# The experts' gathered rows turned by a transposing DMA in place of TensorE

## The chip, the cores and the metric

The kernel runs on one core of a Trainium2 chip. Its time is the device time of one execution in microseconds (us), and what is compared is the median of several runs. A profiled execution gives the trace. TensorE does matrix products and turns tiles (a turn is a product with the identity matrix), VectorE (DVE) and ScalarE (ACT) do elementwise work and read TensorE's results out of its eight banks, GpSimd (POOL) issues the indirect transfers here, SyncE (SP) the plain ones.

## The reference

One decoder layer with three parts, each followed by a residual sum and a layer norm: causal self-attention, cross-attention with rotary positions, and a mixture of experts. The change touches only the last:

```python
x = hidden_states.reshape(-1, 512)                     # 2048 tokens of 512
scores = jax.nn.sigmoid(x @ gate_w.T) + bias
topk_w, topk_idx = jax.lax.top_k(scores, 4)            # 4 of 16 experts for each token
topk_w = topk_w / (jnp.sum(topk_w, axis=-1, keepdims=True) + 1e-20)
cw = jnp.sum(jax.nn.one_hot(topk_idx, 16) * topk_w[..., None], axis=1)
g, u = jnp.einsum('th,eih->eti', x, Wg), jnp.einsum('th,eih->eti', x, Wu)   # 256 wide
zw = jax.nn.silu(g) * u * cw.T[:, :, None]
out = jnp.einsum('eti,ehi->th', zw, Wd)
out = out + jax.nn.silu(x @ Sg.T) * (x @ Su.T) @ Sd.T  # shared expert
```

## The kernel before, in words

Every product is made in three passes of float16: each operand is split into a high and a low half, and high x high, high x low and low x high are summed in a bank (`three_pass`, L284). The profile therefore shows three matmuls, L288, L289 and L290, wherever a product stands.

The stages run one after the other: self-attention, cross-attention, routing with the shared expert, the experts, and a last stage that adds up and normalises. Routing has written the token rows to `scratch_x`; a row there holds 512 high halves, 512 low halves and the four weights of the token. It has also made lists that place the chosen (token, expert) pairs in 79 tiles of 128 rows, each tile of one expert.

The experts' stage (`experts`, L1847) is a loop over these 79 tiles, unrolled, and each engine has its own copy of it. In step s:

- TensorE does the gate and up products of tile s (`gate_and_up`, 12 matmuls) into bank `GU[s % 2]`; turns the rows of tile s + 2, which makes the left operands of a later step (`turn_rows`, L1462, 8 matmuls, high halves into bank `XH`, low halves into `XL`); does the down product of tile s - 1 (`down`, 6 matmuls); and turns z of tile s (`turn_z`, 2 matmuls).
- ScalarE makes silu of the gate (L1948), reads the number of expert weights that must have landed for tile s + 2 and waits for them, copies `XH` to `xth` (L1954), in every second step scales the output of tile s - 1 (L1957), and copies z's high half (L1959).
- VectorE makes z (L1972), copies `XL` to `xtl` (L1976), forms the weights of tile s + 2 (L1979, L1981), scales the outputs of the other steps (L1985), and makes z's low half (L1987).
- GpSimd gathers the rows of tile s + 4 into one of four slots of `rows` (L1456, 128 rows of 2064 bytes), and then sends the scaled output of tile s - 1 to HBM with an accumulating indirect transfer (L1934), which also waits for the accumulating transfer two tiles back.
- SyncE loads expert weights into a ring of four (L1452, 1.5 MB each), each load when the one before has landed and TensorE has done with the slot.

`xth` and `xtl` have two buffers each, so the operands of tile s + 2 go where those of tile s were read. A `Timeline` is a semaphore with an order of events written out by hand: `mark` counts an event, `value` is the count at which it has happened, and the engine marks them in exactly this order. ACT's queue is in order: what stands behind a waiting instruction waits too.

Of the kernel before, what the change touches and what calls it, by code (L numbers as in the profile page):

```python
# [108 lines left out]
def build(nc, x, xT, cT, maskf, wqT, wkT, wvT, b3, woT, bo, xwq, xwk, xwv, xwo,  # L109
# [3 lines left out]
    with top:  # L113
# [3 lines left out]
        def sem(name):  # L117
            return top.enter_context(nc.semaphore(name))
# [1310 lines left out]
        def moe_buffers(where):  # L1429
# [4 lines left out]
            m.rows, m.s_rows = b("rows", [P, 4, ROW], F16), [sem(f"moe_rows{j}") for j in range(4)]  # L1434
            m.xth = [b(f"xth{p}", [P, KD, ST], F16) for p in range(2)]
            m.xtl = [b(f"xtl{p}", [P, KD, ST], F16) for p in range(2)]
            m.list = b("list", [P, COLS], U32)
# [412 lines left out]
        def experts(m, ln):  # L1850
# [3 lines left out]
            with ExitStack() as ctx:  # L1854
# [6 lines left out]
                s_yo = [sem(f"mo_s_yo{j}") for j in range(U)]  # L1861
                XH, XL, GU, ZT, Y = bank[0], bank[1], [bank[2], bank[3]], [bank[4], bank[5]], [bank[6], bank[7]]

# [4 lines left out]
                AC = Timeline(sem("mo_act"), per_step(["si", "xh", "y", "zh"], 1), 0, [], U)  # L1868
                DV = Timeline(sem("mo_dve"), per_step(["z", "xl", "wp", "ws", "y", "zl"], 0), 0, [], U)
                assert LAST.q % 2  # L1870
# [41 lines left out]
                def _(pool):  # L1912
                    routing.gpsimd(pool)
                    routing.wait(pool, routing.PE, "turn1")
                    for s in range(NTILES + 1):
                        st = step(s)
                        if s >= 2 and s + U < NTILES:
                            pool.wait_ge(PE.sem, PE.value("turn", st, 2))
                            pool.wait_ge(DV.sem, DV.value("ws", st, 2))
                        elif s < 2:  # L1920
                            routing.wait(pool, routing.DV, f"ws{s}")
# [18 lines left out]
                def _(act):  # L1940
# [4 lines left out]
                    for s in range(NTILES):  # L1945
                        st, par = step(s), s % 2
                        act.wait_ge(PE.sem, PE.value("gu", st))
                        AC.mark(act.activation(sg[par][:, :], GU[par][:, 0:FI], ACT.Silu, scale=1 / WS), "si", st, () if turns(s) else ("xh",))  # L1948
                        if turns(s):
                            loaded = act.value_load(m.need[0:1, s + 2:s + 3], min_val=16, max_val=16 * NE)  # L1950
                            act.wait_ge(m.s_w, loaded)
                            met(act)
                            act.wait_ge(PE.sem, PE.value("turn", st))
                            AC.mark(act.activation(m.xth[par][:, :, :].rearrange("p k t -> p (k t)"), XH[:, :], ACT.Copy), "xh", st)  # L1954
                        if out_of(st) is AC:
                            act.wait_ge(PE.sem, PE.value("y", st))
                            AC.mark(act.activation(stored(act, s - 1)[:, :], Y[(s + 1) % 2][:, :], ACT.Copy, scale=weight(act, s - 1)), "y", st)  # L1957
                        act.wait_ge(PE.sem, PE.value("zt", st))
                        AC.mark(act.activation(zh[par][:, :, :].rearrange("p n t -> p (n t)"), ZT[par][:, 0:FI], ACT.Copy), "zh", st)  # L1959
# [6 lines left out]
                def _(dve):  # L1966
                    routing.vector(dve)
                    DV.start(dve)
                    for s in range(NTILES):
                        st, par = step(s), s % 2  # L1970
                        dve.wait_ge(AC.sem, AC.value("si", st))
                        i = dve.scalar_tensor_tensor(z[par][:, :], GU[par][:, FI:2 * FI], OS / WS, sg[par][:, :], ALU.mult, ALU.mult)  # L1972
                        DV.mark(i, "z", st, () if turns(s) else ("xl", "wp", "ws"))
                        if turns(s):
                            dve.wait_ge(PE.sem, PE.value("turn", st))
                            i = dve.tensor_copy(m.xtl[par][:, :, :].rearrange("p k t -> p (k t)"), XL[:, :])  # L1976
                            DV.mark(i, "xl", st)
                            t = s + 2
                            DV.mark(dve.tensor_tensor(m.of_pick[:, t % 2, :], weights_of(m, t), m.which[:, t, :], ALU.mult), "wp", st)  # L1979
                            dve.wait_ge(DV.sem, DV.value("wp", st))  # L1980
# [11 lines left out]
                def _(pe):  # L1992
# [7 lines left out]
                    def gate_and_up(s, w):  # L2000
# [5 lines left out]
                        else:  # L2006
                            pe.wait_ge(AC.sem, AC.value("xh", st, 2))
                            pe.wait_ge(DV.sem, DV.value("xl", st, 2))
                        n = 2 * FI
# [4 lines left out]
                        mm = three_pass(pe, GU[par][:, :], pairs[2:], start=False)  # L2014
                        PE.mark(mm, "gu", st, () if turns(s) else ("turn",))
                        return following
# [20 lines left out]
                    for s in range(NTILES):  # L2037
                        st = step(s)
                        following = gate_and_up(s, w)
                        if turns(s):  # L2040
                            t = s + 2
                            if s == 0:
                                routing.wait(pe, routing.DV, "to")
                            pe.wait_ge(m.s_rows[t % U], t // U * 16 + 16)
                            pe.wait_ge(AC.sem, AC.value("xh", st, 1))
                            pe.wait_ge(DV.sem, DV.value("xl", st, 1))
                            mm = turn_rows(pe, m, t % U, XH, XL)
                            PE.mark(mm, "turn", st, ("y",) if s == 0 else ())
                        if s:
# [228 lines left out]
```

## Time and profile before

| | us |
|---|---|
| median of 3 runs | 1805.72 (1804.32 to 1809.44) |
| profiled execution, its time | 1802.7 |
| its span in the trace | 1800.9 |
| TensorE busy | 1703.9 (95%) |
| VectorE busy | 1321.3 (73%) |
| ScalarE busy | 921.6 (51%) |
| GpSimd busy | 892.8 (50%) |
| experts' stage | about 1392 to 1762 |

The 40 slices of the page are 45 us each, so the experts' stage is about slices 32 to 39. A matmul of 512 columns is shown with 379 ns, but matmuls are pipelined: the start of the next one comes 216 ns later, and this distance is what it costs. The DMA share is the mean busy share of the 16 DMA engines that carry all queues.

### The profile page before, as it was taken

What the parts mean: (1) busy time and instruction counts of PE and PEld (TensorE: products, weight loads), DVE (VectorE), ACT (ScalarE), POOL (GpSimd) and SP (SyncE); (2) the same over time, 40 slices, a digit from 0 to 9 for tenths busy, and PEclk for the clock granted to TensorE, in tenths of its full rate; (3) what the DMA queues carried; (4) which work ended last, traced back from release to release, by engine and by line L of the source; (5) the groups of instructions that cost most, each with busy time, mean ns of one, the idle gap of its engine ahead of it and who ended that gap; (6) DMA issues with size and microseconds to landing.
All of it is one profiled execution on the core that took longest, in us unless ns stands there. A gap on an engine that the chain in (4) does not pass through costs nothing. (4 is left out here: it accounts for less than half of the span.)

```text
span 1800.9 us, 38771 instructions
## 1 busy us (share of the span) xinstructions
PE 1703.9 (95%) x15285; PEld 984.0 (55%) x15285; DVE 1321.3 (73%) x2251; ACT 921.6 (51%) x1545; POOL 892.8 (50%) x728
## 2 busy tenths in 40 slices
PE   6999999799999999999999999999899999899990
PEld 4676766455555555555555555555454555455550
DVE  4788789678888888888888888888879444344445
ACT  4566656755646464556465645565631333333335
POOL 7743032554646454646464555465531555455550
PEclk8999999999999999999999999999999999999996
DMA  9620010211413222214122122121244678787668
GB/s 283 143 49 20 8 62 3 95 66 42 141 53 107 77 71 94 89 46 143 53 89 77 53 92 73 48 94 59 77 160 141 153 153 221 201 224 153 116 103 298
DMA packets 84945, 190.40 MB, mean 106 GB/s; under 512 B 10848, under 2 KB 29664, under 8 KB 82720
## 3 DMA queue, kind: packets, MB, share of 16 engines
q1 hardware_dynamic: 61104, 129.44, 21.3%
q0 software_dynamic: 23088, 58.37, 16.0%
q8 instruction: 126, 2.06, 0.5%
q14 instruction: 51, 0.42, 0.1%
q10 hardware_dynamic: 576, 0.11, 0.0%
HBM read 124.68 MB, written 63.21 MB: 104 GB/s over the span
## 5 line engine op out<-in xcount | busy, mean ns | idle before, releaser
L288 PE MATMUL bank<-xhl,front_h 128*128 128x512 f16 x704 | 268.5, 381 | 14.6 <-DVE front_l L408 10.4
L289 PE MATMUL bank<-xhl,front_h 128*128 128x512 f16 x704 | 268.5, 381 | 0.0
L290 PE MATMUL bank<-xhl,front_l 128*128 128x512 f16 x704 | 268.2, 381 | 0.0
L1027 POOL TENSOR_TENSOR xa_xs<-xa_xs,sn 128x512 f32<-128x512 f32 x160 | 234.0, 1462 | 45.7 <-ACT xa_xs L1079 45.7
L1038 POOL TENSOR_TENSOR xa_sc<-xa_sc,xa_rs 128x1024 f32<-128x1024 f32 x32 | 62.3, 1946 | 375.7 <-DVE xa_rs L1278 375.7
L1032 POOL TENSOR_TENSOR xa_rr<-xa_x,xa_xs 128x512 f32<-128x512 f32 x160 | 231.8, 1449 | 12.7 <-DVE xa_x L1183 0.2
L288 PE MATMUL bank<-out_h,xa_oh 128*128 128x512 f16 x512 | 194.8, 380 | 8.8 <-DVE xa_ol L1165 6.6
L1934 POOL DMA_INDIRECT scratch_y<-raw_front,moe_to x79 | 125.3, 1586 | 146.0 <-DVE mo_zl L1987 116.0
L289 PE MATMUL bank<-out_l,xa_oh 128*128 128x512 f16 x512 | 194.8, 380 | 0.0
L290 PE MATMUL bank<-out_h,xa_ol 128*128 128x512 f16 x512 | 194.6, 380 | 0.0
L1078 ACT ACTIVATE xa_xs<-bank 64x512 f32<-64x512 f32 x160 | 95.1, 594 | 131.0 <-PE bank L290 127.3
L1183 DVE TENSOR_TENSOR xa_x<-bank,cs 128x512 f32<-128x512 f32 x160 | 109.5, 686 | 63.8 <-ACT xa_xs L1079 59.1
L1188 DVE TENSOR_TENSOR xa_rql<-xa_rr,xa_rqh 128x512 f16<-128x512 f32 x128 | 141.4, 1105 | 13.4 <-ACT xa_rqh L1085 12.7
L1131 ACT ACTIVATE xa_sc<-xa_sc 128x512 f32<-128x512 f32 x64 | 40.1, 629 | 204.6 <-DVE xa_sc L1203 204.6
L1972 DVE SCALAR_TENSOR_TENSOR raw_out<-bank,raw_out 128x256 f32<-128x256 f32 x79 | 33.6, 425 | 150.0 <-ACT raw_out L1948 150.0
L288 PEld LDWEIGHTS bank<-xhl,front_h 128*128 128x128 f16 x704 | 69.1, 98 | 93.5 <-issue 13.1
L288 PE MATMUL bank<-moe_ring,moe_xth 128*128 x316 | 119.8, 379 | 0.0
L289 PE MATMUL bank<-moe_ring,moe_xth 128*128 x316 | 119.8, 379 | 0.0
L290 PE MATMUL bank<-moe_ring,moe_xtl 128*128 x316 | 119.8, 379 | 0.0
L290 PEld LDWEIGHTS bank<-xhl,front_l 128*128 128x128 f16 x704 | 69.2, 98 | 84.2 <-issue 1.9
L1175 DVE SCALAR_TENSOR_TENSOR acc<-bank,acc 128x512 f32<-128x512 f32 x128 | 85.9, 671 | 37.8 <-PE bank L290 37.7
L289 PEld LDWEIGHTS bank<-xhl,front_h 128*128 128x128 f16 x704 | 69.1, 98 | 78.0 <-issue 1.6
(300 smaller groups left out, 4668.0 us busy)
## 6 DMA issues: line engine op xcount, KB each, us to landing
xa_rawc<-in_ew SPq DMA_DIRECT2D x32, 768.0 KB, 5.7
moe_ring<-scratch_w SPq DMA_DIRECT2D x16, 1536.0 KB, 8.0
scratch_w<-xa_chunk_h SPq DMA_DIRECT2D x32, 384.0 KB, 2.3
scratch_w<-xa_chunk_l SPq DMA_DIRECT2D x32, 384.0 KB, 3.3
raw_front<-in_xwq SPq DMA_DIRECT2D x8, 1024.0 KB, 8.0
raw_out<-in_xwo SPq DMA_DIRECT2D x8, 1024.0 KB, 5.4
scratch_y<-xa_zero SPq DMA_DIRECT2D x18, 256.0 KB, 5.9
acc<-in_x POOLq DMA_DIRECT2D x4, 1024.0 KB, 12.5
```

The costliest lines, as they stand in the source:

```text
L288: pe.matmul(out_ap, ah, bh, start=start and m == 0, stop=False)
L289: pe.matmul(out_ap, ah, bl, start=False, stop=False)
L290: mm = pe.matmul(out_ap, al, bh, start=False, stop=stop and m == n - 1)
L1027: PO.mark(pool.tensor_tensor(xr, xr, sn[:, :].rearrange("p (a s) -> p a s", a=1) .to_broadcast([P, QT // S, S]), ALU.mult), f"sm{r}", st)
L1032: PO.mark(pool.tensor_tensor(rr[r % 2][:, :], x0[r % 3][:, :], xs[r % 3][:, :], ALU.add), f"ra{r}", st)
L1038: PO.mark(pool.tensor_tensor(s4, s4, rs[:, :, :].rearrange("p h (t a) -> p (h t) a", a=1) .to_broadcast([P, 16, S]), ALU.mult), "nm", st)
L1078: act.activation(xs[r % 3][0:64, :], src[64:128, :], ACT.Copy)
L1131: AC.mark(act.activation(s2, s2, ACT.Exp, scale=float(HD2) ** -0.5), f"ex{h}", st, ("ch",) if (i, q, h) == (NG - 1, NQ - 1, 1) else ())
L1175: DV.mark(dve.scalar_tensor_tensor(row, home[f"w{t}"][:, :], 1 / (WS * OS), row, ALU.mult, ALU.add), f"w{t}", st, also)
L1183: DV.mark(dve.tensor_tensor(xr, home_of(r, st)[:, :].rearrange("p (a s) -> p a s", s=S), cs[:, :].rearrange("p (a s) -> p a s", a=1) .to_b ...
L1188: DV.mark(dve.tensor_tensor(rotated(rkl, rql, r), rr[r % 2][:, :].rearrange("p (a s) -> p a s", s=S), rotated(rkh, rqh, r), ALU.subtract), ...
L1934: pool.indirect_dma_start((ya, yb)[t % 2][:, :], bass.IndirectOffsetOnAxis(m.to[:, t:t + 1], 0), y[:, :], None, compute_op=ALU.add).then_i ...
```

## The change

In place of eight turns on TensorE and two copies out of banks, ScalarE issues one transposing DMA for each tile, from the slot in `rows` to a joint buffer `xt`, whose first four blocks are `xth` and whose last four are `xtl`. It is 128 rows of 1024 float16, 256 KB. ScalarE itself now waits for the gather before it issues. TensorE's gate and up products wait for the transposing DMA of two steps before (`mo_turned`), and so does GpSimd before it gathers into the slot again. The wait for the expert weights moves from behind silu to before it. VectorE waits for the gather in its own right.

```diff
--- before.py
+++ after.py
@@ -1432,8 +1432,8 @@
             m = MoeBuffers()
             m.ring, m.s_w = b("ring", [P, RING * 2 * EW], F16), sem("moe_w")
             m.rows, m.s_rows = b("rows", [P, 4, ROW], F16), [sem(f"moe_rows{j}") for j in range(4)]
-            m.xth = [b(f"xth{p}", [P, KD, ST], F16) for p in range(2)]
-            m.xtl = [b(f"xtl{p}", [P, KD, ST], F16) for p in range(2)]
+            m.xt = [b(f"xt{p}", [P, 2 * KD, ST], F16) for p in range(2)]
+            m.xth, m.xtl = [x[:, 0:KD, :] for x in m.xt], [x[:, KD:, :] for x in m.xt]
             m.list = b("list", [P, COLS], U32)
 
             m.bias, m.count, m.count_h = b("bias", [P, NE]), b("count", [P, P]), b("count_h", [P, P], F16)
@@ -1859,14 +1859,15 @@
                 zh, zl = ([b(f"{n}{j}", [P, IB, P], F16) for j in range(2)] for n in ("zh", "zl"))
                 yo = [raw_front[:, j * D:(j + 1) * D] for j in range(U)]
                 s_yo = [sem(f"mo_s_yo{j}") for j in range(U)]
-                XH, XL, GU, ZT, Y = bank[0], bank[1], [bank[2], bank[3]], [bank[4], bank[5]], [bank[6], bank[7]]
+                s_turned = [sem(f"mo_turned{j}") for j in range(2)]
+                GU, ZT, Y = [bank[2], bank[3]], [bank[4], bank[5]], [bank[6], bank[7]]
 
                 def per_step(names, odd):
 
                     return [(q, n) for q in range(U) for n in names if n != "y" or q % 2 == odd]
                 PE = Timeline(sem("mo_pe"), events(["gu", "turn", "y", "zt"], steps=U), 0, [], U)
                 AC = Timeline(sem("mo_act"), per_step(["si", "xh", "y", "zh"], 1), 0, [], U)
-                DV = Timeline(sem("mo_dve"), per_step(["z", "xl", "wp", "ws", "y", "zl"], 0), 0, [], U)
+                DV = Timeline(sem("mo_dve"), per_step(["z", "wp", "ws", "y", "zl"], 0), 0, [], U)
                 assert LAST.q % 2
                 block = ctx.enter_context(nc.Block())
 
@@ -1915,7 +1916,7 @@
                     for s in range(NTILES + 1):
                         st = step(s)
                         if s >= 2 and s + U < NTILES:
-                            pool.wait_ge(PE.sem, PE.value("turn", st, 2))
+                            pool.wait_ge(s_turned[s % 2], s // 2 * 16)
                             pool.wait_ge(DV.sem, DV.value("ws", st, 2))
                         elif s < 2:
                             routing.wait(pool, routing.DV, f"ws{s}")
@@ -1944,14 +1945,16 @@
 
                     for s in range(NTILES):
                         st, par = step(s), s % 2
-                        act.wait_ge(PE.sem, PE.value("gu", st))
-                        AC.mark(act.activation(sg[par][:, :], GU[par][:, 0:FI], ACT.Silu, scale=1 / WS), "si", st, () if turns(s) else ("xh",))
                         if turns(s):
                             loaded = act.value_load(m.need[0:1, s + 2:s + 3], min_val=16, max_val=16 * NE)
                             act.wait_ge(m.s_w, loaded)
                             met(act)
-                            act.wait_ge(PE.sem, PE.value("turn", st))
-                            AC.mark(act.activation(m.xth[par][:, :, :].rearrange("p k t -> p (k t)"), XH[:, :], ACT.Copy), "xh", st)
+                        act.wait_ge(PE.sem, PE.value("gu", st))
+                        AC.mark(act.activation(sg[par][:, :], GU[par][:, 0:FI], ACT.Silu, scale=1 / WS), "si", st, ("xh",))
+                        if turns(s):
+                            t = s + 2
+                            act.wait_ge(m.s_rows[t % U], t // U * 16 + 16)
+                            act.dma_start_transpose(m.xt[par][:, :, :], m.rows[:, t % U, 0:2 * D]).then_inc(s_turned[par], 16)
                         if out_of(st) is AC:
                             act.wait_ge(PE.sem, PE.value("y", st))
                             AC.mark(act.activation(stored(act, s - 1)[:, :], Y[(s + 1) % 2][:, :], ACT.Copy, scale=weight(act, s - 1)), "y", st)
@@ -1970,12 +1973,10 @@
                         st, par = step(s), s % 2
                         dve.wait_ge(AC.sem, AC.value("si", st))
                         i = dve.scalar_tensor_tensor(z[par][:, :], GU[par][:, FI:2 * FI], OS / WS, sg[par][:, :], ALU.mult, ALU.mult)
-                        DV.mark(i, "z", st, () if turns(s) else ("xl", "wp", "ws"))
+                        DV.mark(i, "z", st, () if turns(s) else ("wp", "ws"))
                         if turns(s):
-                            dve.wait_ge(PE.sem, PE.value("turn", st))
-                            i = dve.tensor_copy(m.xtl[par][:, :, :].rearrange("p k t -> p (k t)"), XL[:, :])
-                            DV.mark(i, "xl", st)
                             t = s + 2
+                            dve.wait_ge(m.s_rows[t % U], t // U * 16 + 16)
                             DV.mark(dve.tensor_tensor(m.of_pick[:, t % 2, :], weights_of(m, t), m.which[:, t, :], ALU.mult), "wp", st)
                             dve.wait_ge(DV.sem, DV.value("wp", st))
                             i = dve.tensor_reduce(m.weight[:, t % U:t % U + 1], m.of_pick[:, t % 2, :], AX.X, ALU.add)
@@ -2005,14 +2006,14 @@
                             routing.wait(pe, routing.DV, f"xl{s}")
                         else:
                             pe.wait_ge(AC.sem, AC.value("xh", st, 2))
-                            pe.wait_ge(DV.sem, DV.value("xl", st, 2))
+                            pe.wait_ge(s_turned[par], s // 2 * 16)
                         n = 2 * FI
                         pairs = [(m.xth[par][:, k, :], m.xtl[par][:, k, :], w[:, k * n:(k + 1) * n], w[:, EW + k * n:EW + (k + 1) * n])
                                  for k in range(KD)]
                         three_pass(pe, GU[par][:, :], pairs[:2], stop=False)
                         following = weights(s + 1) if s + 1 < NTILES else None
                         mm = three_pass(pe, GU[par][:, :], pairs[2:], start=False)
-                        PE.mark(mm, "gu", st, () if turns(s) else ("turn",))
+                        PE.mark(mm, "gu", st, ("turn",) if s else ("turn", "y"))
                         return following
 
                     def down(s, w, before=()):
@@ -2037,15 +2038,6 @@
                     for s in range(NTILES):
                         st = step(s)
                         following = gate_and_up(s, w)
-                        if turns(s):
-                            t = s + 2
-                            if s == 0:
-                                routing.wait(pe, routing.DV, "to")
-                            pe.wait_ge(m.s_rows[t % U], t // U * 16 + 16)
-                            pe.wait_ge(AC.sem, AC.value("xh", st, 1))
-                            pe.wait_ge(DV.sem, DV.value("xl", st, 1))
-                            mm = turn_rows(pe, m, t % U, XH, XL)
-                            PE.mark(mm, "turn", st, ("y",) if s == 0 else ())
                         if s:
                             if s == 1:
                                 routing.wait(pe, routing.DV, "y3.3")
```

TensorE, at the end of a gate and up product (`identh` is the identity, `moe_rows` the gathered rows, `mo_zh` z's high half; waits in brackets name semaphores). Before:

```order
L290 MATMUL bank<-moe_ring,moe_xtl 128x512
L1466 MATMUL bank<-identh,moe_rows 128x128 [waits mo_dve,mo_act,moe_rows0]
L1466 MATMUL bank<-identh,moe_rows 128x128 x7
L288 ISA [waits mo_dve,mo_act]
L288 MATMUL bank<-moe_ring,mo_zh 128x512
```

The same place now:

```order
L290 MATMUL bank<-moe_ring,moe_xt 128x512
L288 ISA [waits mo_dve,mo_act]
L288 MATMUL bank<-moe_ring,mo_zh 128x512
L289 ISA
L289 MATMUL bank<-moe_ring,mo_zh 128x512
```

The eight turns are gone, and with them TensorE's wait for the gathered rows.

TensorE, from the turn of z to the next gate and up product, before:

```order
L2031 MATMUL bank<-ident,raw_out 128x128 [waits mo_dve]
L2031 MATMUL bank<-ident,raw_out 128x128
L288 ISA [waits mo_dve,mo_act]
L288 MATMUL bank<-moe_ring,moe_xth 128x512
L289 ISA
```

And now:

```order
L2032 MATMUL bank<-ident,raw_out 128x128 [waits mo_dve]
L2032 MATMUL bank<-ident,raw_out 128x128
L288 ISA [waits mo_turned1,mo_act]
L288 MATMUL bank<-moe_ring,moe_xt 128x512
L289 ISA
```

The gate and up product waits for `mo_turned1`, the transposing DMA, where it waited for VectorE's copy.

ScalarE, one step in which it also scales an output (`moe_need` holds the counts of landed weights, `raw_out` here is silu, `raw_front` the scaled output). Before:

```order
L1948 ACTIVATE raw_out<-bank 128x256 [waits mo_pe]
L1950 TENSOR_LOAD moe_need
L1950 ISA x2
L1954 ACTIVATE moe_xth<-bank 128x512 [waits moe_w,mo_pe]
L1957 ACTIVATE raw_front<-bank,moe_weight 128x512 [waits mo_dve,mo_s_yo0,mo_pe]
L1959 ACTIVATE mo_zh<-bank 128x256 [waits mo_pe]
```

Now:

```order
L1949 TENSOR_LOAD moe_need
L1949 ISA x2
L1953 ACTIVATE raw_out<-bank 128x256 [waits moe_w,mo_pe]
L1957 DMA_TRANSPOSE moe_xt<-moe_rows 128x8x128 [waits moe_rows3]
L1960 ACTIVATE raw_front<-bank,moe_weight 128x512 [waits mo_dve,mo_s_yo0,mo_pe]
L1962 ACTIVATE mo_zh<-bank 128x256 [waits mo_pe]
```

The transposing DMA stands between silu and the scaled output and waits for the gathered rows; silu now stands behind the wait for the weights (`moe_w`).

## Rows read from the trace of the kernel before

**Rows 1.** The page, busy time and slices of the span.

```profile
PE 1703.9 (95%) x15285; PEld 984.0 (55%) x15285; DVE 1321.3 (73%) x2251; ACT 921.6 (51%) x1545; POOL 892.8 (50%) x728
...
PEclk8999999999999999999999999999999999999996
DMA  9620010211413222214122122121244678787668
```

**Rows 2.** Busy time by engine in two stretches; columns PE, PEld, DVE, ACT, POOL.

```profile
1400.00:1500.00 100.00, 100.00 (x617) 53.96 (x616) 43.93 (x122) 36.31 (x78) 55.84 (x44) 1.00 0.71 146
1500.00:1600.00 100.00, 94.26 (x573) 50.29 (x572) 41.25 (x115) 34.17 (x73) 52.52 (x41) 1.00 0.86 230
```

**Rows 3.** Timeline, TensorE, one step; start, duration.

```profile
1453.62 0.61 PE L1466 MATMUL bank<-identh,moe_rows 128*128 128x128 f16 x8
1454.07 0.38 PE L288 MATMUL bank<-moe_ring,mo_zh 128*128 x1
...
1458.17 0.61 PE L1466 MATMUL bank<-identh,moe_rows 128*128 128x128 f16 x8
```

**Rows 4.** Timeline, all engines, the same step; in brackets idle before.

```profile
1451.03 0.38 PE L288 MATMUL bank<-moe_ring,moe_xth 128*128 x1
...
1453.82 0.39 ACT L1948 ACTIVATE raw_out<-bank 128x256 f32<-128x256 f32 x1 [2.21 <-PE bank L290]
...
1455.57 0.69 ACT L1957 ACTIVATE raw_front<-bank,moe_weight 128x512 f32<-128x512 f32 x1 [0.50 <-PE bank L290]
...
1456.15 0.38 ACT L1959 ACTIVATE mo_zh<-bank 128x256 f16<-128x256 f32 x1
1456.56 0.42 DVE L1987 TENSOR_TENSOR mo_zl<-bank,mo_zh 128x256 f16<-128x256 f32 x1 [1.04 <-ACT mo_zh L1959]
1457.05 1.59 POOL L1934 DMA_INDIRECT scratch_y<-raw_front,moe_to  x1 [1.60 <-DVE mo_zl L1987]
...
1458.94 0.99 POOL L1456 DMA_INDIRECT moe_rows<-scratch_x,moe_list  x1 [0.30 <-PE bank L1466]
```

**Rows 5.** Groups by line, 1400 to 1748 us; busy, mean ns, idle before.

```profile
L1976 DVE CAST moe_xtl<-bank 128x512 f16<-128x512 f32 x75 | 51.0, 681 | 0.4 <-PE bank L1466 0.4
L1954 ACT ACTIVATE moe_xth<-bank 128x512 f16<-128x512 f32 x75 | 44.8, 597 | 32.4 <-PE bank L1466 19.5 <-DMA moe_ring<-scratch_w 12.9
```

**Rows 6.** DMA, 1461 to 1497 us: queue, MB, share; issues, us to landing.

```profile
q0 software_dynamic: 1843, 4.33, 68.0%
...
scratch_y<-raw_front,moe_to POOLq DMA_INDIRECT x8, 4.9
moe_rows<-scratch_x,moe_list POOLq DMA_INDIRECT x8, 4.5
```

**Rows 7.** DMA, 1451 to 1460 us, beside one load of weights.

```profile
q1 hardware_dynamic: 143, 1.57, 54.1%
q0 software_dynamic: 331, 0.79, 41.7%
...
scratch_y<-raw_front,moe_to POOLq DMA_INDIRECT x2, 7.6
moe_rows<-scratch_x,moe_list POOLq DMA_INDIRECT x2, 6.4
```

**Rows 8.** DMA, 1344 to 1364 us, loads of weights in 12 KB rows.

```profile
q1 hardware_dynamic: 816, 4.19, 57.3%
```

**Rows 9.** DMA, 124.5 to 134.2 us, the mask's load.

```profile
q0 software_dynamic: 288, 1.05, 64.3%
```

**Rows 10.** DMA, 1364 to 1370 us, a store in pieces of 16 bytes.

```profile
q1 hardware_dynamic: 2064, 0.03, 15.9%
...
scratch_x<-moe_w SPq DMA_DIRECT2D x1, 32.0 KB, 4.1
```

**Rows 11.** Timeline around the longer of two waits for weights.

```profile
1554.04 0.38 ACT L1948 ACTIVATE raw_out<-bank 128x256 f32<-128x256 f32 x1 [2.21 <-PE bank L290]
1560.40 0.60 ACT L1954 ACTIVATE moe_xth<-bank 128x512 f16<-128x512 f32 x1 [5.98 <-DMA moe_ring<-scratch_w]
...
1562.55 0.39 PE L288 MATMUL bank<-moe_ring,mo_zh 128*128 x1 [0.85 <-DVE mo_zl L1987]
```

**Rows 12.** Timeline, SyncE in the experts' stage, and one load.

```profile
1405.59 226.18 SPq L1452 DMA_DIRECT2D moe_ring<-scratch_w  x12
...
1451.08 0.33 SPq L1452 DMA_DIRECT2D moe_ring<-scratch_w  x1
```

## Prediction

> **What bounds the kernel now.** I read the page first. TensorE is busy 95% of the span at full granted clock, and the DMA engines, light until then, go to 6 to 8 tenths in the experts' stage [rows 1]. Then the windows of that stage: TensorE has no idle time at all in 1400 to 1500 us and some in 1500 to 1600 us, where the DMA share is 0.86 [rows 2]. No other engine is above 60%. Then one step in the timeline. From one block of turns to the next it takes 1458.17 - 1453.62 = 4.55 us, and the next matmul behind the turns starts 0.45 us after them (1454.07 - 1453.62) [rows 3]. So eight turns cost 0.45 us of the engine that sets the pace, and a step without them takes at least 4.10 us.
>
> Two more engines matter because they get new work. ScalarE waits most of a step for TensorE [rows 4]. The DMA engines are the ones to watch. In a stretch without loads of weights, 8 steps in 36 us, the software queue alone keeps them busy for 68.0%, that is 3.1 us of each step, for one gather and one accumulating store [rows 6]. A load of weights by itself moves 4.19 MB in 57.3% of 20 us, 366 GB/s, so its 1.57 MB take 4.3 us [rows 8]. Twelve of them fall in this stage [rows 12]. Beside one, two steps need 2 x 3.1 + 4.3 = 10.5 us of DMA time as priced apart, but the window of 9 us shows 54.1% + 41.7%, 8.6 us busy [rows 7]. Crowded queues are packed tighter, by a factor of 0.83, and the engines are full there.
>
> **What goes.** 77 of the 79 steps have turns, 77 x 0.45 = 34.7 us of TensorE, all on the path. The copies, 681 ns on VectorE and 597 ns on ScalarE [rows 5], lie beside matmuls. Removing them is worth nothing unless TensorE waits for what stands behind them, and here it doesn't in a quiet step.
>
> **What comes: time on the path of a tile.** Step s begins at 1451.03 in the step shown. Silu ends at 1453.82 + 0.39 = 1454.21, so the transposing DMA can be issued 3.18 us into the step [rows 4]. Its result is needed when step s + 2 begins. With steps of 4.10 us that leaves 8.20 - 3.18 = 5.0 us from issue to landing, with today's 4.55 us it leaves 5.9 us. Up to 5.0 us the whole 34.7 us are won; at 5.9 us nothing is; each further us costs half a us in a step. The nearest rows are the two indirect transfers of the same 256 KB: 4.5 and 4.9 us in quiet steps [rows 6], 6.4 and 7.6 us beside a load [rows 7]. Quiet steps would just do, steps beside a load would not.
>
> **What comes: DMA time.** 256 KB for each tile, and how much of the 16 engines it takes no row shows. Fine end of the cost: the rate of the weights' load gives 0.262 MB / 366 GB/s = 0.72 us [rows 8]. Coarse end: if the turned data is written in pieces of 32 bytes (my assumption, 8192 of them), the store of 2064 small packets, 15.9% of 6 us = 0.95 us, gives 0.95 x 8192 / 2064 = 3.8 us [rows 10]. I take the mask's load, the nearest row whose source is cut into short runs (256 bytes in HBM): 1.05 MB in 64.3% of 9.7 us is 168 GB/s, so 1.56 us [rows 9].
>
> Quiet steps (77 - 2 x 12 = 53): 3.1 + 1.56 = 4.64 us of DMA time as priced apart, 3.9 us packed by 0.83. The step cannot be under 4.10, so it lies between 4.10 and 4.64; I take the middle, 4.37: 53 x -0.18 = -9.5 us. Steps beside a load (24): (2 x 4.64 + 4.3) x 0.83 = 11.3 us for two, 5.64 us each: 24 x 1.09 = +26 us. The path of a tile says nearly the same: (3.18 + 7.6) / 2 = 5.4 us.
>
> The Trainium skill bears on this price. "DMA: Bandwidth & Descriptors", section "Latency and other measured facts", gives a transposing DMA 261 GB/s, and 350 to 400 in the contiguous case. By it 256 KB would take an estimated 0.66 to 1.0 us, and the sum would end at about the fast rival below. No run here shows it yet.
>
> **The other edits.** ScalarE's issue: between the 0.33 us of a plain issue [rows 12] and the 1.59 us of the indirect one [rows 4]. Behind it stand the scaled output (0.69), z's high half (0.38) and then VectorE's low half (0.42), which TensorE wants at 4.10 + 2.60 = 6.70 us. 3.18 + x + 0.69 + 0.38 + 0.42 = 4.67 + x, so it is free up to x = 2.0 us; no cost. ScalarE's new wait for the gather: TensorE had the same wait 0.6 us earlier, so no cost. GpSimd's gather now waits for the transposing DMA of two tiles back. From the scaled output, GpSimd needs 0.8 us, 1.59, 0.30 and 0.99, 3.7 us of a step [rows 4]; it fits in 4.10, barely. The wait for weights ahead of silu: it was long twice. In the one shown, ScalarE went on at 1560.40 and TensorE began its down product at 1562.55, with the next gate and up product already done [rows 11]. Now silu waits as well, z is turned at about 1561.3, the gate and up product takes 2.60 more, and the down product begins at 1563.9: 1.35 us later, twice, +2.7 us. Idle time of ScalarE for weights was 12.9 us in all [rows 5], so more than some 5 us it can't be; at least it costs nothing.
>
> Sum: -9.5 + 26 + 2.7 = +19 us on the profiled execution's 1802.7, so 1822. The median of the runs is 3.0 us above that execution; I predict 1824 us.
>
> **Rivals.**
>
> A, it is hidden, faster. At 0.72 us of DMA time quiet steps need 3.8 us and run at 4.10: 53 x -0.45 = -23.9. Beside a load (2 x 3.8 + 4.3) x 0.83 = 9.9, 4.94 each: +9.4. With the +2.7: -12, so 1794. If the steps beside loads run at 4.10 too, 1774. For it: an unhindered landing leaves room, and even beside the loads of 1500 to 1600 us TensorE idles under 6 us in 100 today [rows 2]. Against it: 0.86 DMA share before anything is added [rows 2]. It turns from faster to slower at about 1.1 us of DMA time per tile.
>
> B, the transposing DMA is much slower than a copy, and sets the step by itself. At 3.8 us quiet steps take 5.7 (packed) to 6.9 us, steps beside loads 7.5: 53 x 1.15 to 2.3, + 24 x 2.95, + 2.7 = +135 to +196, so 1940 to 2000. For it: pieces that small cost almost as much time as large ones [rows 10]. Against it: the engines took only 0.95 us for 2064 of them. The Trainium skill, "VectorE: DVE Perf Modes", section "The three transpose paths", has 1309 ns for one 128 x 128 block by DMA and 390 ns on TensorE. Eight blocks one after the other would be an estimated 10.5 us, steps of (3.18 + 10.5) / 2 = 6.8 us, about 1980 us. Of TensorE the trace disagrees: a turn costs 0.45 / 8 = 56 ns here [rows 3].
>
> C, ScalarE's sequencer is held by the issue beyond 2.0 us, so that z's halves come late. At 2.5 us a step takes 4.6 us: -34.7 + 77 x 0.5 + 2.7 = +7, 1812; at 2.4 us it is no change. Against it: the dearest issue in the rows is 1.59 us.
>
> **How the numbers follow.** Forecast 0.38, A 0.36, B 0.14, C and an even sum of gain and loss 0.12. The forecast's own range is 1808 to 1860. The range of 1776 to 1925 takes in A but for its best case, and most of the way to B. A measurement of this kernel can tell 0.3%, about 5 us, from no change. Faster is A, 0.36; no change is the last case, 0.12; slower is the forecast with B, 0.52.
>
> **What would show it.** In the profile after: turns and copies gone; quiet steps (the distance of z's turns) of 4.3 to 4.4 us; steps beside a load of 5 to 6 us with TensorE waiting at the first gate and up matmul for the transposing DMA; DMA share above 0.9 all through the stage; landing of the transposing DMA about 5 us in quiet steps and over 7 beside a load; ScalarE's issue under 2 us. The forecast is wrong if quiet steps stand at 4.10 and the loads add under 0.4 us a step (A), if every step is over 5.5 us (B), or if TensorE waits for z's halves (C).

## The result and the profile after

| | before | after |
|---|---|---|
| median of 4 runs each, us | 1805.02 | 1939.15 |
| ratio (95% interval) | | 1.0721 (1.0693 to 1.0748) |
| profiled execution: its time, its span, us | 1802.7, 1800.9 | 1932.74, 1930.9 |

The change makes the kernel 7% slower. The forecast was 1824 us in a range up to 1925, slower by a seventh of what came. One of the four runs after (1972.07 us) and two of the five of e6 below, its traced one among them, were in a slower state of the chip, so the differences below go by the other runs, with a median of 1933 us after (128 us slower) and 1890 us for e6. The page after, against [rows 1]:

```profile
PE 1706.6 (88%) x14669; PEld 955.5 (49%) x14669; DVE 1276.0 (66%) x2174; ACT 875.5 (45%) x1468; POOL 892.1 (46%) x728
...
PEclk9999999999999999999999999999979879899986
DMA  9610101122232231321212212024499989999898
...
q10 hardware_dynamic: 81888, 20.30, 9.6%
```

The busy time of TensorE didn't fall, though 616 turns are gone, and its granted clock dips in the experts' stage. The transposing DMA is queue q10: 1056 packets a tile, nearly all of 256 bytes. What TensorE and GpSimd waited for, 1400 to 1880 us (total, times, longest):

```profile
PEld bank L288 <- issue: 168.0, 124, 23.5
PE bank L288 <- DMA moe_xt<-moe_rows: 118.2, 20, 23.2
POOL moe_rows L1456 <- DMA moe_xt<-moe_rows: 35.2, 11, 12.2
```

118 us of waits for the transposing DMA in 20 portions, one of them 23 us. (The first row counts largely the same waits, seen by the weight loads.) Three stretches, against [rows 2] (length, busy PE, PEld, DVE, ACT, POOL, then granted clock, DMA share, GB/s):

```profile
1400.00:1425.00 25.00, 9.17 (x45) 4.34 (x43) 3.29 (x12) 2.50 (x6) 5.22 (x4) 0.76 1.11 60
1475.00:1500.00 25.00, 19.87 (x95) 9.29 (x94) 6.11 (x19) 5.42 (x13) 11.88 (x9) 1.00 1.05 216
1825.00:1850.00 25.00, 22.38 (x108) 10.65 (x106) 7.05 (x24) 5.95 (x14) 13.12 (x11) 1.00 1.05 154
```

The last one has no load of weights in it. Two turns of z, the first and the last over such steps:

```profile
1752.95 0.38 PE L2032 MATMUL bank<-ident,raw_out 128*128 128x128 f32 x2
...
1879.46 0.38 PE L2032 MATMUL bank<-ident,raw_out 128*128 128x128 f32 x2
```

Between them lie 23 steps, 5.50 us each on average: mostly three of some 4.1 to 4.8, then one of 6.4 to 11.6 in which TensorE waits. The first stretch is another thing: DMA engines busy 111% by their records (queues overlap) while 60 GB/s move. Its timeline:

```profile
1404.93 0.34 SPq L1452 DMA_DIRECT2D moe_ring<-scratch_w  x1
...
1407.78 16.72 ACTq L1957 DMA_TRANSPOSE moe_xt<-moe_rows  x1
...
1424.61 0.69 ACT L1960 ACTIVATE raw_front<-bank,moe_weight 128x512 f32<-128x512 f32 x1 [16.47 <-issue]
...
1432.40 0.60 PE L288 MATMUL bank<-moe_ring,moe_xt 128*128 x1 [23.23 <-DMA moe_xt<-moe_rows]
```

A load of weights is issued, and 3 us later the issue of one transposing DMA holds ScalarE's queue for 16.7 us (1.3 us is the median of all 77). TensorE stands for 23 us. The DMA engines meanwhile, 1409 to 1429.5 us, in 40 slices:

```profile
DMA  9900899689999999997334314994222546899869
GB/s 47 39 0 0 38 56 31 25 46 56 57 45 52 55 35 56 92 96 50 35 14 34 38 13 43 54 95 42 26 26 26 38 46 150 309 313 334 305 288 342
...
q10 hardware_dynamic: 554, 0.13, 55.0%
q0 software_dynamic: 140, 0.39, 41.7%
q1 hardware_dynamic: 105, 1.24, 15.8%
```

For 17 us some 43 GB/s, then at once over 300: the load was there to be moved and wasn't. For the first 9 of these 17 us the records show the engines busy nearly throughout, after that mostly for a third of the time.

After such a wait the matmuls come at half rate (chain of waits, start, duration):

```profile
1716.76 0.61 PE bank L288
1717.37 0.43 PE bank L289
1717.79 0.43 PE bank L290
```

The granted clock from 1716.80 to 1720.20 us is 0.53: 0.43 us apart is the 1.2 GHz level; 0.22 us, as before, is the 2.4 GHz one. The engine had stood idle for 7 us before. The groups of 1400 to 1880 us show how much that is (count, busy us, mean ns):

```profile
L288 PE MATMUL bank<-moe_ring,moe_xt 128*128 x301 | 125.9, 418 | 127.4 <-DMA moe_xt<-moe_rows 118.2 <-issue 7.9 <-ACT mo_zh L1962 0.6
L289 PE MATMUL bank<-moe_ring,moe_xt 128*128 x301 | 124.6, 414 | 0.0
L290 PE MATMUL bank<-moe_ring,moe_xt 128*128 x300 | 123.5, 412 | 0.0
```

Against 379 ns each, 39 + 35 + 33 = 107 ns x 300 = 32 us of shown duration. A slow one shows about 0.24 us more and costs 0.21 more, so the clock takes some 28 us, a fifth of the 128. That is worked out from rows; no run isolates it.

### The profile page after: what moved, and what is told of

The parts are those of the page before. It is cut to its first block and busy times, and to the rows that moved or that the text cites. A ratio compares the mean times of both kernels' runs of the same rounds, so it can differ in the third digit from the quotient of the medians.

```text
span 1930.9 us, 37460 instructions
## 1 busy us (share of the span) xinstructions
PE 1706.6 (88%) x14669; PEld 955.5 (49%) x14669; DVE 1276.0 (66%) x2174; ACT 875.5 (45%) x1468; POOL 892.1 (46%) x728
## 5 line engine op out<-in xcount | busy, mean ns | idle before, releaser
L1027 POOL TENSOR_TENSOR xa_xs<-xa_xs,sn 128x512 f32<-128x512 f32 x160 | 233.7, 1460 | 45.8 <-ACT xa_xs L1079 45.8
L288 PE MATMUL bank<-moe_ring,moe_xt 128*128 x316 | 131.6, 416 | 127.8 <-DMA moe_xt<-moe_rows 118.2
L1953 ACT ACTIVATE raw_out<-bank 128x256 f32<-128x256 f32 x79 | 30.3, 383 | 297.9 <-PE bank L290 271.9
L289 PE MATMUL bank<-moe_ring,moe_xt 128*128 x316 | 130.3, 412 | 0.0
L290 PE MATMUL bank<-moe_ring,moe_xt 128*128 x316 | 129.5, 410 | 0.0
L288 PEld LDWEIGHTS bank<-moe_ring,moe_xt 128*128 128x128 f16 x316 | 32.7, 104 | 184.7 <-issue 168.0
L288 PEld LDWEIGHTS bank<-xhl,front_h 128*128 128x128 f16 x704 | 69.1, 98 | 91.8 <-issue 13.0
L1456 POOL DMA_INDIRECT moe_rows<-scratch_x,moe_list x79 | 78.1, 988 | 75.3 <-DMA moe_xt<-moe_rows 35.2
```

Source lines behind the costliest of these rows:

```text
L288: pe.matmul(out_ap, ah, bh, start=start and m == 0, stop=False)
L289: pe.matmul(out_ap, ah, bl, start=False, stop=False)
L290: mm = pe.matmul(out_ap, al, bh, start=False, stop=stop and m == n - 1)
L1027: PO.mark(pool.tensor_tensor(xr, xr, sn[:, :].rearrange("p (a s) -> p a s", a=1) .to_broadcast([P, QT // S, S]), ALU.mult), f"sm{r}", st)
L1456: pool.indirect_dma_start(m.rows[:, t % 4, :].bitcast(F32), None, xs[:, :].bitcast(F32), bass.IndirectOffsetOnAxis(m.list[:, t:t + 1], 0)) ...
```

## The experiments

My theory once the result was seen: the transposing DMA is a dearer and touchier transfer than its bytes say, with a cost in every step and another beside loads. The rivals: only the bytes count; or it is merely late, and nobody else suffers.

**m1, transfers by themselves.** A kernel of its own; each transfer, or each four in a row, is awaited before a tiny instruction on ScalarE.

> A kernel of its own, which leaves the whole layer out: 256 KB transposing DMAs on ScalarE's queue, each waited for, in five phases: alone; four in a row; beside pairs of a gather and an accumulating store of 256 KB; beside loads of 1.5 MB; beside both. Plain copies of the same bytes, pairs and a load are also run alone. Theory (the transposing DMA is a dearer and touchier transfer than its bytes say): alone 3 to 4 us from issue to landing, in a row 2.0 to 2.4 us each; beside pairs 6 to 8 us; beside a load over 10 us, more than the load takes (8 us). Rival (only bytes count): in a row 0.7 to 1.6 us each, beside pairs under 6 us, beside a load under 8 us, and plain copies within 20% of the transposing ones.

Timeline of ScalarE, the first alone, the second beside pairs, the third beside a pair and a 1.5 MB load (in brackets the wait):

```profile
45.23 0.20 ACT L83 ACTIVATE tick_act<-tick_act 128x1 f32<-128x1 f32 x1 [3.10 <-DMA xt<-rows]
...
122.48 0.20 ACT L83 ACTIVATE tick_act<-tick_act 128x1 f32<-128x1 f32 x1 [6.46 <-DMA xt<-rows]
...
187.30 0.20 ACT L83 ACTIVATE tick_act<-tick_act 128x1 f32<-128x1 f32 x1 [14.64 <-DMA xt<-rows]
```

Alone 3.1 us; four in a row 7.5, so 1.5 us for each further one (2.0 to 2.4 were expected: a miss). Beside pairs of a gather and an accumulating store 6.3 to 6.8 us; beside a load alone 7.5 and 6.4 (over 10 expected, another miss); beside both 14.6, about twice that, though this is a single transfer, the one issued together with the load. The next took 7.9. In the window of one alone:

```profile
q10 hardware_dynamic: 1056, 0.26, 44.4%
```

44.4% of 3.07 us is 1.36 us of all engines, under my 1.56. A plain copy of the same bytes lands in 2.3 us, and the share of its queue in that time is 30.2%: 0.70 us of all engines, half of 1.36.

**e1 and e2, small loads, after and before; e3, plain copies.**

```diff
-                        expert_weights(sp, m, e)
+                        o = (e % RING) * 2 * EW
+                        sp.dma_start(m.ring[:, o:o + 64], ews[e * P:(e + 1) * P, 0:64]).then_inc(m.s_w, 16)
```

```diff
-  act.dma_start_transpose(m.xt[par][:, :, :], m.rows[:, t % U, 0:2 * D]).then_inc(s_turned[par], 16)
+  act.dma_start(m.xt[par][:, :, :].rearrange("p k t -> p (k t)"), m.rows[:, t % U, 0:2 * D]).then_inc(s_turned[par], 16)
```

> The changed kernel with 12 of the 16 loads of expert weights cut to 16 KB, so that most tiles are computed with weights that are not theirs. Theory (stalls beside loads are a term of their own, some 80 us): 1850 to 1870 us, steps of 5.2 to 5.6 us. Rival (the transfer is slow everywhere, and loads only add their own DMA time): less than 30 us under the changed kernel's 1939, over 1905.

> The kernel before with the same loads cut: the control. Loads cost it the stalls of 1550 to 1620 us, about 14 us of TensorE's waits: 1785 to 1798 us by either theory.

> The changed kernel with a plain copy of the same 256 KB in place of the transposing one, so the operands are not turned. Theory (it is the transposing): TensorE's steps return to 4.1 to 4.4 us, 1775 to 1810 us. Rival (any 256 KB more a step does it, since the DMA engines were 0.7 to 0.9 busy): 1880 us and more.

1849.03, 1797.03 and 1829.15 us. e1 and e2 came as the theory said (e1 a microsecond under its range). The plain copy is neither: 24 us slower than before (1.0129, 1.0114 to 1.0143) where the theory had it faster or even, yet 104 us under the changed kernel. In e1 the step is still 5.23 us on average. One queue's record of 1700 to 1745 us there:

```profile
q10 hardware_dynamic: 10131, 2.52, 38.4%
```

10131 / 1056 = 9.6 tiles in 17.3 us: 1.80 us of all engines each, beside gathers and stores, where it takes 1.36 alone.

**e12, plain copies with small loads,** run later with e10 and e11, completes a table of two by three.

> Plain copies in place of the transposing DMAs (operands not turned) and small loads (most tiles with weights not theirs): what the loads cost a plain copy is 1829 less this. If loads hurt only transposing DMAs: 1815 to 1825 us. If they hurt any third stream: 1775 to 1790 us, quiet steps of 4.3 us all through.

| us | TensorE turns | plain copy | transposing DMA |
|---|---|---|---|
| whole loads | 1805 | 1829 | 1933 |
| small loads | 1797 | 1785 | 1849 |
| loads cost | 8 | 44 | 84 |

The two right columns differ in the form of the transfer alone. Transposing adds 40 us to the price of the loads and costs 64 us without them, together the 104. From the left column to the middle one more than a stream of 256 KB a step is new: the turns are gone, and silu stands behind the wait for weights. The loads' 36 us more belong to all of this together. In e3's trace TensorE waits 26.1 us for the copies, in 8 portions, and twice for a late z, 9.3 us, while ScalarE waits for weights.

e12 also shows what the turns are really worth. With small loads and a cheap copy the step is not 4.10 but 4.36 us on average. One of its steps, TensorE and its weight loads:

```profile
1700.59 0.29 PEld L2033 LDWEIGHTS bank<-ident,raw_out 128*128 128x128 f32 x2 [0.19 <-DVE raw_out L1976]
...
1700.73 0.38 PE L2033 MATMUL bank<-ident,raw_out 128*128 128x128 f32 x2
...
1702.03 0.38 PE L290 MATMUL bank<-moe_ring,moe_xt 128*128 x1
1702.47 0.10 PEld L288 LDWEIGHTS bank<-moe_ring,moe_xt 128*128 128x128 f16 x1 [0.56 <-issue]
1702.47 0.39 PE L288 MATMUL bank<-moe_ring,moe_xt 128*128 x1
```

The weights' load for z's turn waits 0.19 us for z, but this costs no time: the turn itself starts 0.22 us after the matmul before it, as matmuls do in a running stream. The cost is in the middle of the gate and up product, where the program reads the next ring place into a register. There the next matmul starts 0.44 us after the last and not 0.22, and the step takes 4.34 us. The kernel before has no gap at this place, so the turns had covered it. How they did isn't shown.

**m2, beside what, and how many at once.**

> A second kernel of its own, the layer left out: five transposing DMAs, each waited for, beside gathers alone; five beside accumulating stores alone; twelve, four in flight, beside pairs of both; plain copies, each waited for, beside pairs, and beside pairs and a 1.5 MB load; eight transposing ones, four in flight, beside a load alone. Theory A (DMA time is what is short): with four in flight they come out no faster than one by one, 5 to 6 us each beside pairs. Theory B (one transfer is slow because its pieces wait for each other, while the engines have time left): four in flight come out at 2.5 to 4 us each. Plain copies beside pairs 3 to 4 us by both, under 7 beside pairs and a load.

Beside gathers alone 4.4 to 5.7 us, beside accumulating stores 4.7 to 5.3, beside both (m1) 6.3 to 6.8. Four in flight beside both:

```profile
99.43 0.20 ACT L64 ACTIVATE tick_act<-tick_act 128x1 f32<-128x1 f32 x1 [12.31 <-DMA xt<-rows]
```

The next four took 15.28: 3.1 and 3.8 us each, half of one by one but over twice the 1.5 alone. So theory B holds for the latency, and still leaves a rate of about 3 to 4 us a tile. Four in flight beside a load alone took 11.19 us, 2.8 each. Plain copies beside pairs took 4.3 to 5.1 us in the crowded part, and 8.95 for the one beside a pair and the load (14.6 for a transposing one); both are more than expected. So a plain copy, too, takes twice its 2.3 us beside two streams: what transposing adds is 3.1 in place of 2.3 us alone and 6.3 to 6.8 in place of 4.3 to 5.1 beside pairs.

**e4, turns kept, and the DMA added for nobody.**

```diff
+ act.wait_ge(m.s_rows[t % U], t // U * 16 + 16)
+ if s >= 2:
+     act.wait_ge(s_turned[par], s // 2 * 16)
+ act.dma_start_transpose(m.spare_xt[par][:, :, :], m.rows[:, t % U, 0:2 * D]).then_inc(s_turned[par], 16)
```

> The kernel before, with TensorE's turns and the copies kept, and the transposing DMA added for each tile into buffers that nothing reads. If the damage is done only by late landing (theory B), TensorE doesn't wait for it and the time is 1805 to 1825 us, of which the loads' lateness makes the most. If the DMA engines are over-full (theory A), gathers and loads come late too and it is 1860 to 1920 us.

1906.98 us (1.0537, 1.0489 to 1.0584), as theory A said. Nothing reads the turned data, so what TensorE waits for is something else:

```profile
ACT raw_front L1965 <- issue: 79.9, 12, 18.8
PEld bank L1467 <- DMA moe_rows<-scratch_x,moe_list: 72.9, 18, 20.9
PE bank L1467 <- DMA moe_rows<-scratch_x,moe_list: 65.1, 13, 20.4
...
DMA to landing us min/median/max: 3.1/6.6/31.0
```

TensorE waits up to 20 us for a gather, and ScalarE stands 80 us ahead of its scaled outputs, in 12 portions, where its own issues are: eleven of the issues took over 2 us, the longest 19.2. 102 us are lost though TensorE never waits for the result. Two other waits for it remain: ScalarE's before the next issue into the same buffer (in the edit above), and GpSimd's before it gathers into the slot again. A part of the 102 us may be these waits, so the run doesn't show by itself that the DMA engines were over-full. The last line is of the 77 transposing DMAs: half of them took over 6.6 us from issue to landing.

**e5, only the high halves by DMA.** Low halves stay on TensorE with bank `XL` and VectorE's copy.

> Only the high halves turned by DMA (128 KB a tile), the low halves on TensorE as before: four turns, 0.22 us of TensorE's 0.45, stay. By both theories the quiet steps nearly fit (landing about 5 us for a budget of 5.2) and stalls beside loads are about half: 1825 to 1870 us. Under 1800 would say that size matters more than linearly.

1868.67 us (1.0355, 1.0290 to 1.0421), within the expectation: half the bytes, 64 us of the 128. Its late steps without loads are 4.50 us apart. The median landing is 5.2 us, and the median issue 1.24 us, for half the bytes nearly the same as for all.

**e6, three buffers and five slots.**

```diff
- if turns(s):
-     t = s + 2
-     act.wait_ge(m.s_rows[t % U], t // U * 16 + 16)
-     act.dma_start_transpose(m.xt[par][:, :, :], m.rows[:, t % U, 0:2 * D]).then_inc(s_turned[par], 16)
+ if s + 3 < NTILES:
+     turn_by_dma(act, s + 3)          # into xt[s % 3], from one of five slots
```

> The changed kernel with three turned buffers in place of two and five slots for gathered rows in place of four, each tile turned three steps ahead: 4.1 us more for each transposing DMA to land. Theory B: quiet steps go to 4.1 to 4.4 us and stalls beside loads lose 3 to 4 us each, 1810 to 1860 us. Theory A: quiet steps stay at 5.2 us, 1915 to 1940 us.

1889.51 us (1.0452, 1.0402 to 1.0503), between the two. Late steps without loads fall from 5.50 to 4.58 us: there it was the latency. Stalls beside loads stay, with steps of up to 26.6 us. The two longest, 21 us each, are no waits of TensorE for the transposing DMA: one is for z's high half, with ScalarE standing where it issues, the other for z, with ScalarE waiting for weights. Even with all the time it needs, the step is no shorter than TensorE's own 4.55.

**e7, e8, e9, loads cut into six, one after the other; e10, e11, six at once.**

```diff
+ for c in range(6):
+     done = sp.dma_start(m.ring[:, o + c * n:o + (c + 1) * n], ews[e * P:(e + 1) * P, c * n:(c + 1) * n])
    ...  # cut: e7 to e9 wait here for the piece, e10 and e11 wait for all six behind the loop
```

> The changed kernel with each of the 12 loads of weights cut into six of 256 KB, each issued when the one before has landed, so that less of a load is queued at a time. If the stalls come of a transposing DMA caught between a whole load and the indirect transfers (theory), they shrink by half: 1939 to 1885 to 1905 us. If they are just the DMA time of the same bytes (rival), 1925 us and more, since six loads take longer to land than one.

> The same cut on top of three turned buffers and five slots (1891 us with whole loads). Theory: 1820 to 1855 us, stalls beside loads under 4 us each. Rival: 1880 us and more. Neither expects it under the kernel before, since quiet steps of this version take 4.6 us.

> The kernel before with the same cut, as a control. Loads cost it 9 us in all (1806 against 1797 with small loads). Landing later, the two long waits for weights grow by 5 us or so each: 1806 to 1818 us. Under 1803 would make it the best version.

> The changed kernel with each load of weights as six transfers of 2 KB rows, all issued at once: as much queued, in shorter rows. If the amount counts: 1930 to 1950 us, as the changed kernel. If the long rows count, the stalls shrink: 1860 to 1905 us.

> The control, the kernel before with the same six transfers at once: 1803 to 1812 us by either.

1922.43, 1915.10, 1864.19, 1903.13 and 1806.71 us. Pacing was a poor test: it costs the kernel before 59 us, since weights come late, where I expected 1 to 13. e7 came between its two ranges, and e8 missed the theory's range by 60 us, on the rival's side. What can be read is the difference between after and before: 128 us with whole loads, 58 with paced ones, 52 with small ones. (Waits for late weights may hide waits for the transposing DMA, so this is a hint and no more.)

e10 against e11 is clean, 96 us in place of 128, where the same cut costs TensorE's kernel 2 us: six transfers with rows of 2 KB in place of one with rows of 12 KB take 32 us off, at the upper edge of what I expected if row length were all. Its trace says which part they take away. The first line has the length of an issue on ScalarE's queue (shortest, median, longest, in ns), the second TensorE's waits:

```profile
L1964 ACTq DMA_TRANSPOSE moe_xt<-moe_rows x77: 1247/1302/2977, 1398.2 to 1854.5; - x77
...
PE bank L288 <- DMA moe_xt<-moe_rows: 86.5, 24, 7.8
```

No issue holds ScalarE for more than 3.0 us now (16.7 in the changed kernel), and no wait is longer than 7.8 us (23.2). Beside whole loads of 12 KB rows no issue of e3's plain copies took over 0.53 us, and none of e5's transposing DMAs of half the bytes over 2.5. So the long standstill was seen only with long rows and whole transposing DMAs of 256 KB together. The shorter waits remain. Issuing the transposing DMAs from another engine's queue was not tried. It would have told the held queue from the late landing.

No version with all its work beats the kernel before: e2 and e12, the only ones under it, leave out weights, and e12 the turning too.

## Why the prediction was wrong

The forecast was the sum -9.5 + 26 + 2.7 = +19 us; it came to +128. The direction and the two places, ordinary steps and steps beside loads, were the named ones. What sets an ordinary step was not: I priced it by DMA time, and it is the landing time. Both sizes were far off.

- **The price in DMA time, 1.56 us a tile.** Measured 1.36 alone and 1.80 beside the other queues. The number held, in part by luck: the mask's load that I took it from moves 1.05 MB in 288 packets, 3.6 KB each, and the transposing DMA in pieces of 256 bytes and less. Taking it for all there is to a transfer did not hold. A plain copy takes 0.70 us, which is close to rival A's 0.72. By the same working it would come out at 1794 us, and e3 measured 1829. So the sum was short for a plain copy too, and that e3's +24 us is near my +19 is chance.
- **Quiet steps, 4.37 us, -9.5 us in all.** This is the first step that failed. Measured 5.23 in e1, 0.68 over today's 4.55 where I had 0.18 under it, and over all 77 steps +52 us (1849 - 1797). I took the landing time from the indirect transfers, 4.9 us [rows 6], against a budget of 5.0, so that it cost nothing, and let DMA time set the step. By the formula (3.18 + L) / 2 the measured step says L = 7.3 us on average, though in the trace the wait comes whole in one step of four or so. m1 has 6.3 to 6.8 beside pairs, and e4 a median of 6.6, loads included. e6 shows that landing was the limit: with a step more to land in, the steps fell to 4.58 us with the same bytes. The transposing DMA doubles its time beside two other streams (so does a plain copy, from 2.3 us). A row of a transfer that already lives beside the others was no measure for one that is added to them.
- **Beside loads, +26 us.** Measured 84 - 8 = +76 for what loads add. I spread the DMA time of a load evenly over 24 steps, packed by 0.83. That packing was seen with two queues; with the third the rate fell to 43 GB/s for 17 us. The table says 40 us of it belong to the transposing and 36 to what plain copies bring as well. Why so little moves then isn't settled: pieces with shorter rows take away 32 us and the longest stalls, so length of rows, or the size of one transfer, is part of it.
- **Eight turns, 0.45 us a step, all on the path.** Wrong by more than half: 4.36 us in e12, not 4.10. They covered the register read in the gate and up product. I asked what was behind the removed copies and not what ran under the removed turns.
- **ScalarE's issue, free up to 2.0 us.** The issue itself is 1.3 us, so in ordinary steps that held. Beside whole loads it holds the queue up to 16.7 us. Rival C named the place but saw a constant price.
- **The clock** was no term at all. Behind waits such as that of 7 us TensorE's matmuls run at the 1.2 GHz level; about 28 us, worked out above.
- **The weights' wait ahead of silu, +2.7 us:** no run isolates it. In the trace after, TensorE waits twice for z, 3.7 and 2.3 us, where ScalarE stood waiting for weights; before, its two waits of that kind were 2.5 and 1.9 us; the first is that of [rows 11]. That is 1.7 us more, and 9.3 in place of 4.4 in e3.

Rival B gave 1940 to 2000 us, and 1933 to 1939 came, but not by its way: the engines' time per tile is 1.4 to 1.8 us and not 3.8. The time agrees by chance. What was said for B, that small pieces cost almost as much time as large ones, its rows don't bear out: 0.95 us of 16 engines for 2064 pieces is 7 ns of one engine each [rows 10], against 225 ns for each of the 816 pieces of the weights' loads [rows 8]. The Trainium skill's 261 to 400 GB/s ("DMA: Bandwidth & Descriptors", "Latency and other measured facts") stands against 0.262 MB / 1.36 us = 193 GB/s here, alone and contiguous. The Trainium skill's 1309 ns for one block ("VectorE: DVE Perf Modes", "The three transpose paths") can't be multiplied: eight blocks land in 3.1 us. The measurements decide.

## What to carry to other kernels

Before work goes from an engine to the DMA queues, time that very transfer beside the streams it will run with: alone it took 3.1 us, beside two streams 6.5, and the one beside a bulk load as well 14.6. A plain copy of the same bytes in its place tells apart what the bytes cost and what their form costs. And what is taken off the pacing engine is worth its time only less what it had covered.

## What the runs showed of the hardware

- A transposing DMA of 128 x 1024 float16 from and to SBUF: 1056 packets, mostly of 256 bytes; 1.25 us of the issuing queue; 3.1 us to land alone; 1.5 us each in a row; 1.36 us of the 16 engines, where a plain copy of the bytes takes 0.70.
- Beside gathers and accumulating stores it landed in 6.3 to 6.8 us, a plain copy in 4.3 to 5.1.
- Beside loads with 12 KB rows one issue held ScalarE's queue for 16.7 us, and everything behind it. With 2 KB rows the longest was 3.0 us.
- Beside gathers, accumulating stores and a 1.5 MB load, the 16 engines moved some 43 GB/s for 17 us, in the first 9 of which their records show them busy, then over 300 GB/s.
- After idling 7 us TensorE started six matmuls 0.43 us apart in place of 0.22, at a granted clock of 0.53.
